# A deformable convolution's sampling loop: TensorE samples between its two distance products, and reads copied offsets

## The chip, the cores and the metric

The kernel runs on one core of one Trainium2 chip. The metric is the device time of one execution in microseconds (us), from the first to the last instruction of the core and what lies around them. TensorE (PE), VectorE (DVE), ScalarE (ACT), GpSimd (POOL) and SyncE (SP) run their own streams of instructions and wait for each other on semaphores.

## The reference

The input is 8 images of 64 channels and 32 x 32 pixels. Two deformable convolutions with 3 x 3 taps come first, then a windowed attention and a mixture of experts. The change touches the two deformable convolutions only:

```python
def deform_conv(x, offset, weight, stride, pad, dil):          # dil = 2, pad = 2
    dy = offset[:, 0::2]
    dx = offset[:, 1::2]
    ...
    ys = base_y[None, None, :, None] + (ky * dil)[None, :, None, None] + dy
    xs = base_x[None, None, None, :] + (kx * dil)[None, :, None, None] + dx
    ...                                   # four neighbours, weighted by the fractions of ys and xs
    return jnp.einsum('oik,bikhw->bohw', weight.reshape(Co, Ci, KK), sampled)
off1 = conv2d(x, w_off1, b_off1, stride=1, pad=1)
out = jax.nn.relu(bn_inf(deform_conv(x, off1, w_dc1, 1, 2, 2), g1, beta1, m1, v1))
off2 = conv2d(out, w_off2, b_off2, stride=1, pad=1)
out = bn_inf(deform_conv(out, off2, w_dc2, 1, 2, 2), g2, beta2, m2, v2)
out = jax.nn.relu(out + x)
```

A bilinear sample at a fractional place is a sum over source pixels with the weight (1 - |y distance|) (1 - |x distance|), where that is positive. The kernel computes it so, as a matrix product.

## The kernel before, in words

**Stages.** Convolution 1, convolution 2, layer norm, attention, layer norm, experts. Each deformable convolution first computes its 18 offsets per pixel on PE (line 548). The offsets are split in three bf16 parts, written to memory and read back (lines 610 and 616) into a buffer `off` with the layout that the sampling wants, in two halves of 16 image rows; the semaphores `moved[0]` and `moved[1]` tell of them. If no offset is as large as 2 pixels (a flag that all engines load), the sampler below runs.

**The sampler.** The source is cut in tiles of 4 x 8 pixels: 8 tile rows (TR) by 4 tile columns. A hardware loop of 8 iterations on PE (line 180) takes one tile row each, and inside it nine steps are written out, one per tap. ACT, DVE and POOL have the same work written out without a loop. A step on PE issues:

- **x**, `columns_near` (line 130): four matmuls that turn the offsets of a tap into x distances of each pixel from a tile's columns. ACT takes their absolute value from PSUM (line 247), DVE makes min(|d|, 1) - 1 of it (line 312).
- **y**, `rows_near` (line 149): two matmuls for the y distances; ACT line 256, DVE line 315.
- **S**, the sampling (line 214): 32 matmuls of 32 source pixels by 64 output channels, each recorded in two passes, so 64 records. The moving operand is `s`, the product of the two hats that DVE makes in two pieces (line 327).
- **w**, `weighted_near` (line 111): the source pixels times the weights of three taps, the stationary operand of S; ACT copies it out of PSUM (line 238). Only the steps 0, 4, 5, 6, 7 and 8 of nine have a w.

Steps run ahead: step t makes x and y of tap t+2. x, y and w pass through two PSUM slots in turn, so the k-th of them waits until ACT has emptied the (k-2)-th. On DVE the order per tap n is fixed: hat of x(n+1), hat of y(n+1), then the two products `s` of tap n (function `sampler_dve`, `hats(n + 1)` and then `weights(n)`). Before step 0 of an iteration PE clears four banks of output (line 195), after ACT has copied the previous tile row's sums (line 297) and DVE has added them to `tokens` (line 351); convolution 2 has a further DVE pass there (line 1332).

**Names.** `emptied` counts ACT's passes, `s_ready` DVE's products, `sampled` the S groups, `staged` POOL's copies of source tiles (line 374). Ten items (x and y of the taps 0 and 1, and the first x of others) are made before the loop, after both `moved` waits.

Of the kernel before, what the change touches and what calls it, by code (L numbers as in the profile page):

```python
# [17 lines left out]
P = 128  # L18
# [99 lines left out]
def columns_near(nc, m, cv, k, tap, row, n, i=None):  # L118

    _, cols, ahead = window(cv)  # L120
    kx = tap % 3
    for late in range(2):
        wide = 2 * cv.reach if late else TILE_COLS
        first = tap * PIX + row * W + ahead - 2 * kx + TILE_COLS * late
        for g in range(2):
            src = m.off_flat[:, first:first + n * W] if i is None else tile_rows(m.off_flat, first, n, i)
            src = src.rearrange("p (r c w) -> p r c w", c=TC, w=TILE_COLS) if i is None else src.rearrange(
                "p r (c w) -> p r c w", c=TC)
            dst = slot_banks(m, k)[:, g, 0:n * TC * cols].rearrange("p (r c w) -> p r c w", c=TC, w=cols)
            last = nc.tensor.matmul(dst[:, :, :, TILE_COLS * late:TILE_COLS * late + wide],  # L130
                                    m.near_sel[:, 6 + ((ahead * 3 + kx) * 2 + late) * 2 + g, :], src[:, :, :, 0:wide],
# [4 lines left out]
def tile_rows(off_flat, first, n, i):  # L136

    room = (TAPS * PIX + OFF_TAIL - first) // W * W
    return off_flat[:, first:first + room].rearrange("p (r c) -> p r c", c=W)[:, bass.ds(i * TILE_ROWS, n), :]

def rows_near(nc, m, cv, k, tap, row, i=None):

    n = window(cv)[0]
    first = tap * PIX + row * W
    for g in range(2):
        src = m.off_flat[:, first:first + n * W] if i is None else tile_rows(m.off_flat, first, n, i)
# [8 lines left out]

# [1619 lines left out]
```

## Time and profile before

| | us |
|---|---|
| median of 3 runs | 966.86 |
| lowest and highest | 961.87, 967.53 |
| profiled execution | 967.68 |
| its span | 965.7 |
| convolution 1, first S to last S | 208.4 |
| convolution 2, first S to last S | 267.9 |

The profile is one execution. An engine's busy time counts instructions and not waits; matmul ends are modelled and overlap the next start, so the distance between two starts tells what a group costs. A line of the timeline gives start, duration, engine, source line, what is written and read, and in brackets how long the engine had been idle and what ended it. The granted clock is 1.00 at 2.4 GHz and 0.50 at 1.2 GHz. The two sampling loops are the same code and take 208.4 and 267.9 us.

### The profile page before, as it was taken

To read this page: it belongs to the slowest core of one execution; us is meant where nothing else is said; L and a number is where in the kernel's file an instruction comes from. 1 tells how busy PE (TensorE), PEld (TensorE's weight loads), DVE (VectorE), ACT (ScalarE), POOL (GpSimd) and SP (SyncE) were. 2 spreads that over 40 slices of the span, in tenths; PEclk is the share of its full clock that TensorE was granted. 3 is DMA by queue.
4 is the path that set the end of the run, shared out by engine and by line. 5 is a ranking of instruction groups with operands and counts; after the bars stand their busy time and mean duration, and the time that the engine had idled before them with its cause. 6 is when DMAs were issued, how large, how long until landed. Compare 5 with 4: busy or idle time off the path is not lost.

```text
span 965.7 us, 39200 instructions
## 1 busy us (share of the span) xinstructions
PE 744.0 (77%) x17378; PEld 563.6 (58%) x17378; DVE 538.7 (56%) x993; ACT 452.1 (47%) x750; POOL 166.6 (17%) x200
## 2 busy tenths in 40 slices
PE   6477777777685676676676676699999999999546
PEld 2255555555423454354354345589999999999434
DVE  2465666656534445445455456346666666666843
ACT  1355556565634544444353453335554444454441
POOL 4000000000000000000000003244444444443210
PEclk8789999999997977888887896789999999999779
DMA  8400000000022000000000006100000000000002
GB/s 208 89 4 1 0 1 0 0 1 0 2 41 37 5 3 5 5 4 5 4 4 4 4 5 157 45 1 2 1 0 0 0 0 0 0 0 0 1 0 89
DMA packets 8146, 17.56 MB, mean 18 GB/s; under 512 B 2149, under 2 KB 6117, under 8 KB 7605
## 3 DMA queue, kind: packets, MB, share of 16 engines
q1 hardware_dynamic: 8022, 15.74, 6.6%
q8 instruction: 98, 1.61, 0.7%
q14 instruction: 26, 0.21, 0.1%
HBM read 11.87 MB, written 3.87 MB: 16 GB/s over the span
## 4 chain that ended last, share of the span: by engine, by line
PE 65%; ACT 13%; DVE 9%; issue 8%; DMA 3%; POOL 1%; SPq 1%; ACTq 0%; DVEq 0%
PE banks L214 13%; PE banks L111 9%; ACT y L238 7%; PE banks L778 7%; PE banks L762 6%; PE banks L808 6%; PE banks L149 5%; PE banks L548 4%; PE banks L819 3%; DVE s L327 3%; PE banks L798 3%; ACT hy L256 2%; PE banks L773 2%; PE banks L195 2%; PE banks L130 2%
## 5 line engine op out<-in xcount | busy, mean ns | idle before, releaser
L214 PE MATMUL banks<-s,y 32*64 32x96 f32 (+2 forms) x9216 | 155.6, 262 | 20.0 <-DVE s L327 16.9
L214 PEld LDWEIGHTS banks<-s,y 32*64 32x64 f32 x9216 | 130.2, 141 | 65.0 <-DVE s L327 39.1
L238 ACT COPY y<-banks 128x768 f32<-128x768 f32 x106 | 84.4, 800 | 153.3 <-PE banks L111 153.3
L327 DVE TENSOR_TENSOR s<-hy,y 128x384 f32<-128x384 f32 x288 | 146.8, 552 | 0.1
L312 DVE TENSOR_SCALAR y<-y 128x384 f32<-128x384 f32 x144 | 51.7, 359 | 150.9 <-ACT y L247 150.8
L149 PE MATMUL banks<-off,near_sel 128*128 (+1 forms) x296 | 63.2, 299 | 75.5 <-ACT y L238 64.8
L247 ACT ACTIVATE y<-banks 128x384 f32<-128x384 f32 x160 | 78.3, 493 | 78.6 <-PE banks L130 77.7
L256 ACT ACTIVATE hy<-banks,row_bias 128x512 f32<-128x512 f32 x148 | 101.6, 686 | 22.1 <-PE banks L149 22.0
L374 POOL COPY stage<-src 128x128 f32<-128x128 f32 x72 | 18.9, 306 | 497.0 <-PE banks L111 497.0
L111 PE MATMUL banks<-w_dc,stage 64*32 64x192 f32 x3392 | 98.5, 343 | 4.5 <-ACT y L238 4.5
L130 PE MATMUL banks<-off,near_sel 128*128 (+2 forms) x640 | 60.7, 225 | 48.5 <-issue 28.4
L876 ACT COPY hy<-banks 128x512 f32<-128x512 f32 x64 | 37.7, 589 | 115.9 <-PE banks L808 115.9
L130 PEld LDWEIGHTS banks<-off,near_sel 128*128 128x128 f16 x640 | 40.8, 105 | 87.6 <-issue 80.8
L315 DVE TENSOR_SCALAR hy<-hy 128x512 f32<-128x512 f32 x144 | 61.5, 427 | 53.7 <-ACT hy L256 53.1
L980 POOL TENSOR_TENSOR y<-y,stats 128x1024 f32<-128x1024 f32 x33 | 62.8, 1903 | 143.7 <-DVE stats L921 143.7
L762 PE MATMUL banks<-src,s 128*128 (+1 forms) x560 | 75.3, 279 | 1.1 <-ACT src L699 1.1
L911 DVE TENSOR_REDUCE stats<-banks 128x16 f32<-128x1024 f32 x34 | 41.6, 1225 | 57.5 <-PE banks L778 57.4
L778 PEld LDWEIGHTS banks<-src,y 128*128 128x128 f32 x544 | 68.9, 199 | 5.4 <-issue 0.6
L762 PEld LDWEIGHTS banks<-src,s 128*128 128x128 f32 x560 | 69.4, 196 | 1.5 <-ACT src L699 1.5
L149 PEld LDWEIGHTS banks<-off,near_sel 128*128 128x128 f16 x296 | 17.7, 100 | 88.6 <-issue 84.7
L778 PE MATMUL banks<-src,y 128*128 128x128 f32 x544 | 68.9, 282 | 0.0
L808 PE MATMUL banks<-y,hy 128*128 128x128 f32 x512 | 67.7, 275 | 0.0
(147 smaller groups left out, 1015.7 us busy)
## 6 DMA issues: line engine op xcount, KB each, us to landing
src<-in_x_dram SPq DMA_DIRECT2D x4, 578.0 KB, 5.8
y<-in_w_dram SPq DMA_DIRECT2D x1, 2080.0 KB
off<-in_w_dram SPq DMA_DIRECT2D x2, 1024.0 KB
out_dram<-tokens SPq DMA_DIRECT2D x4, 512.0 KB, 2.6
offsets_dram<-tokens SPq DMA_DIRECT2D x32, 54.0 KB
off<-offsets_dram SPq DMA_DIRECT2D x16, 108.0 KB
near_sel<-in_near_sel_dram SPq DMA_DIRECT2D x1, 960.0 KB
w_dc<-in_w_dc_dram SPq DMA_DIRECT2D x2, 288.0 KB, 10.3
```

The source lines that it names most:

```text
L111: last = nc.tensor.matmul(m.ps[32 * j:32 * j + 32, FIRST_BANK + 2 * (k % 2) + g, (col % 2) * 192:(col % 2) * 192 + 192], m.stage[rows, ima ...
L130: last = nc.tensor.matmul(dst[:, :, :, TILE_COLS * late:TILE_COLS * late + wide], m.near_sel[:, 6 + ((ahead * 3 + kx) * 2 + late) * 2 + g, ...
L149: last = nc.tensor.matmul(dst if i is None else dst.rearrange("p (r c) -> p r c", c=W), m.near_sel[:, tap // 3 * 2 + g, :], src, start=Tru ...
L214: last = nc.tensor.matmul(out[:, r0:r0 + n, first:first + width], m.yk[32 * j:32 * j + 32, ky, g, col, kx * C:(kx + 1) * C], s_rows(m, cv, ...
L238: nc.scalar.copy(m.yk[:, ky, :, 2 * part:2 * part + 2, :].rearrange("p g a n -> p g (a n)"), slot_banks(m, k)[:, :, 0:384]).then_inc(cv.em ...
L247: nc.scalar.activation(block, slot_banks(m, k)[:, :, 0:n * cols].rearrange("p g (r n) -> p g r n", n=cols), ACT.Abs).then_inc(cv.emptied, 1)
L256: nc.scalar.activation(y_rows(m, cv, n).rearrange("p r g c -> p g r c"), slot_banks(m, k)[:, :, 0:rows * W].rearrange("p g (r c) -> p g r ...
L327: nc.vector.tensor_tensor(dst.rearrange("p r g (a c) -> p (r g) a c", a=TC), y, x.rearrange("p r g (a c) -> p (r g) a c", a=TC), ALU.mult) ...
L762: last = nc.tensor.matmul(m.ps[:, hg, h * P:(h + 1) * P], at.a_heads[:, hg * H4 + h, :], at.xh[:, bass.ds(i + b // BLOCKS, 1), first:first ...
L778: last = nc.tensor.matmul(m.ps[:, 2 + bank, first:first + 2 * KEYS], at.g[:, b % 2, hg, j, :], at.pair_windows[:, b % 2, j, :, :], start=F ...
L808: last = nc.tensor.matmul(m.ps[:, 6, j * P:(j + 1) * P], at.xw[:, b % 2, image, j, :], at.pt[:, image, j * P:(j + 1) * P], start=True, sto ...
L980: nc.gpsimd.tensor_tensor(p, p, scale.unsqueeze(2).to_broadcast([P, 2 * TILES * HG, KEYS]), ALU.mult).then_inc(at.probs_ready, 1)
```

## The change

Five edits, all in the sampler:

1. PE's step is x, S, y, w in place of x, y, S, w.
2. POOL copies the window of offsets that a step needs (3 to 8 rows with a margin) into a small buffer `near_off`, nine copies per tile row. PE waits for them (`off_near`). The addresses of x and y no longer depend on the loop's counter, so the address instructions for them go.
3. x and y read 20 rows of one 32-row group each, where they read all 128 partitions with zeros in the selecting operand. The selecting operand halves (30 to 15 versions).
4. w makes 64 x 64 tiles: 8 matmuls where there were 16 of 64 x 32. The images are assigned to partitions in another order, and `stage` is laid out for it.
5. PE and the flag no longer wait for `moved`; POOL waits for `moved[0]` before its first copy, and for `moved[1]` before the first that needs rows of the second half. ACT waits for the offsets' write-out before it overwrites that memory, in tile row 0.

```diff
-IMAGES = [[0, 1, 2, 3], [5, 4, 7, 6]]
+IMAGES = [[0, 2, 1, 3], [5, 7, 4, 6]]
-OFF_TAIL = 160
+OFF_HEAD, OFF_TAIL = 16, 160
+MARGIN = 4
-VERSIONS, NEAR_VERSIONS = 17, 30
+VERSIONS, NEAR_VERSIONS = 17, 15
...
 def weighted_near(nc, m, cv, k, ky, part):
     for col in (2 * part, 2 * part + 1):
-        for j in range(4):
+        for half in range(2):
             for g in range(2):
-                image = IMAGES[g][j]
+                image = IMAGES[g][2 * half]
                 rows = slice(C * (image % 2), C * (image % 2) + C)
                 last = nc.tensor.matmul(
-                    m.ps[32 * j:32 * j + 32, FIRST_BANK + 2 * (k % 2) + g, (col % 2) * 192:(col % 2) * 192 + 192],
-                    m.stage[rows, image // 2, col, :], cv.w_dc[rows, 3 * ky:3 * ky + 3, :],
-                    start=True, stop=True, skip_group_check=True)
+                    m.ps[C * half:C * half + C, FIRST_BANK + 2 * (k % 2) + g, (col % 2) * 192:(col % 2) * 192 + 192],
+                    m.stage[rows, col, 2 * g:2 * g + 2, :].rearrange("p a n -> p (a n)"),
+                    cv.w_dc[rows, 3 * ky:3 * ky + 3, :], start=True, stop=True, skip_group_check=True)
...
-def rows_near(nc, m, cv, k, tap, row, i=None):
+def rows_near(nc, m, cv, k, tap):
     n = window(cv)[0]
-    first = tap * PIX + row * W
     for g in range(2):
-        src = m.off_flat[:, first:first + n * W] if i is None else tile_rows(m.off_flat, first, n, i)
-        dst = slot_banks(m, k)[:, g, 0:n * W]
-        last = nc.tensor.matmul(dst if i is None else dst.rearrange("p (r c) -> p r c", c=W),
-                                m.near_sel[:, tap // 3 * 2 + g, :], src, start=True, stop=True, skip_group_check=True)
+        part = group_rows(g, 0)
+        last = nc.tensor.matmul(slot_banks(m, k)[:, g, 0:n * W], m.near_sel[part, tap // 3, :],
+                                m.near_off[part, tap, MARGIN:MARGIN + n * W], start=True, stop=True,
+                                skip_group_check=True)
     last.then_inc(cv.filled, 1)
...
 def sampler_pe(nc, pe, m, cv):
     old = 2 * cv.reach
-    for half in range(HALVES):
-        pe.wait_ge(cv.moved[half], MOVES)
     for k, item in enumerate(FIRST_COORDS, len(FIRST_WEIGHTED)):
         kind, tap, tile_row = item
         pe.wait_ge(cv.emptied, k - 1)
+        pe.wait_ge(cv.off_near, tap + 1)
...
         for t in range(TAPS):
-            later, tap = divmod(t + AHEAD, TAPS)
+            tap = (t + AHEAD) % TAPS
             pe.wait_ge(cv.emptied, i * PER_ROW + (k - 1))
-            columns_near(nc, m, cv, k, tap, new_rows(cv, tap) + TILE_ROWS * later, TILE_ROWS, i)
-            k += 1
-            pe.wait_ge(cv.emptied, i * PER_ROW + (k - 1))
-            rows_near(nc, m, cv, k, tap, first_row(cv, tap) + TILE_ROWS * later, i)
+            pe.wait_ge(cv.off_near, i * TAPS + (t + AHEAD + 1))
+            columns_near(nc, m, cv, k, tap, old, TILE_ROWS)
             k += 1
...
-            if t in STEP_WEIGHTED:
-
-                pe.wait_ge(cv.emptied, i * PER_ROW + (k - 1))
-                if STEP_WEIGHTED[t] == (0, 0, 1):
-                    pe.wait_ge(cv.staged, i * PAIRS + 2 * PAIRS)
...
             last.then_inc(cv.sampled, 1)
+            pe.wait_ge(cv.emptied, i * PER_ROW + (k - 1))
+            if t in STEP_WEIGHTED:
+
+                pe.wait_ge(cv.emptied, i * PER_ROW + k)
+                if STEP_WEIGHTED[t] == (0, 0, 1):
+                    pe.wait_ge(cv.staged, i * PAIRS + 2 * PAIRS)
+            rows_near(nc, m, cv, k, tap)
+            k += 1
             if t in STEP_WEIGHTED:
                 weighted_near(nc, m, cv, k, *STEP_WEIGHTED[t][0:2])
...
 def sampler_pool(nc, pool, m, cv):
-    for tile_row in range(1, TR + 1):
-        pool.wait_ge(cv.filled, EMPTIED_AT["w", 2, 1, tile_row - 1])
-        stage_pool(nc, m, cv, min(tile_row, TR - 1))
+    rows = window(cv)[0]
+    moved = 0
+    for n in range(TR * TAPS + AHEAD):
+        tile_row, tap = divmod(n, TAPS)
+        if tile_row:
+            pool.wait_ge(cv.filled, EMPTIED_AT["y", tap, tile_row - 1])
+        row = TILE_ROWS * tile_row + first_row(cv, tap)
+        first = row * W - MARGIN
+        left_out = max(-first, 0)
+        if moved == 0 or moved == 1 and row + rows >= HALF_ROWS:
+            pool.wait_ge(cv.moved[moved], MOVES)
+            moved += 1
+        at = OFF_HEAD + tap * PIX + first
+        size = rows * W + 2 * MARGIN
+        nc.gpsimd.tensor_copy(m.near_off[:, tap, left_out:size], m.off_flat[:, at + left_out:at + size]
+                              ).then_inc(cv.off_near, 1)
+        if tap == AHEAD - 1 and tile_row:
+            pool.wait_ge(cv.filled, EMPTIED_AT["w", 2, 1, tile_row - 1])
+            stage_pool(nc, m, cv, min(tile_row, TR - 1))
...
+                if cv.k == 0:
+                    nc.gpsimd.memset(m.near_off[:, :, :], 0.0).then_inc(near_cleared, 1)
+                    pool.wait_ge(near_cleared, 1)
...
-                pe.wait_ge(cv.moved[0], MOVES)
                 pe.wait_ge(cv.flag_ready, 1)
```

ACT's and DVE's instructions and their order stay as they were. On PE, step 4 of an iteration (a step with a w) stood so before, from its y to the x of step 5:

```order
L149 ISA [waits c0_emptied]
L149 MATMUL banks<-off,near_sel 128x256 x2
L199 REGISTER_ALU
L201 REGISTER_ALU [waits c0_emptied]
L205 REGISTER_ALU [waits c0_staged]
L214 MATMUL banks<-s,y 64x8x10 [waits c0_s_ready]
L214 MATMUL banks<-s,y 64x8x10 x7
L214 MATMUL banks<-s,y 64x8x12 x16
L214 MATMUL banks<-s,y 64x8x10 x8
L111 MATMUL banks<-w_dc,stage 32x192 x16
L184 REGISTER_ALU
L130 ISA [waits c0_emptied]
```

The same place of the changed kernel (L195 is S now, L141 is y, L112 is w):

```order
L130 MATMUL banks<-near_off,near_sel 128x16x4 x2
L186 REGISTER_ALU
L195 MATMUL banks<-s,y 64x8x10 [waits c0_s_ready]
L195 MATMUL banks<-s,y 64x8x10 x7
L195 MATMUL banks<-s,y 64x8x12 x16
L195 MATMUL banks<-s,y 64x8x10 x8
L200 REGISTER_ALU
L203 REGISTER_ALU [waits c0_emptied]
L205 ISA [waits c0_emptied]
L141 MATMUL banks<-near_off,near_sel 128x256 [waits c0_staged]
L141 MATMUL banks<-near_off,near_sel 128x256
L112 MATMUL banks<-w_dc,stage 64x192 x8
```

The y that stood ahead of S stands behind it, with the waits that S had, and w has half the instructions.

On DVE the order per tap is the same in both. In the changed kernel (L305 is the hat of x, L308 the hat of y, L320 the products `s`), in the loop's first steps:

```order
L305 TENSOR_SCALAR y<-y 128x384 [waits c0_emptied]
L308 TENSOR_SCALAR hy<-hy 128x512 [waits c0_emptied]
L320 TENSOR_TENSOR s<-hy,y 128x384 [waits c0_hats,c0_sampled]
L320 TENSOR_TENSOR s<-hy,y 128x384
L305 TENSOR_SCALAR y<-y 128x384 [waits c0_emptied]
```

The products of tap n stand behind the hat of y(n+1), as before.

## Rows read from the trace of the kernel before

**Rows 1.** Waits of PE in the whole execution: waiting line, releaser, total us, times, longest.

```profile
PE banks L149 <- ACT y L238: 64.8, 81, 0.8
PE banks L130 <- issue: 28.4, 7, 4.3
```

**Rows 2.** Busy time per engine, first S to last S of each convolution; PEclk is the granted clock.

```profile
53.07:261.46 208.39, 158.79 (x6503) 109.31 (x6503) 125.62 (x286) 121.40 (x201) 8.40 (x32) 0.99 0.00 1
307.25:575.16 267.91, 185.87 (x6504) 123.19 (x6503) 134.05 (x310) 121.57 (x201) 8.40 (x32) 0.84 0.02 4
```

**Rows 3.** Timeline of a step with a w in convolution 1: start, us, engine, line.

```profile
122.36 0.39 PE L149 MATMUL banks<-off,near_sel 128*128 x2 [0.82 <-ACT y L238]
...
122.74 0.99 PE L214 MATMUL banks<-s,y 32*64 32x96 f32 x64
122.78 0.69 ACT L256 ACTIVATE hy<-banks,row_bias 128x512 f32<-128x512 f32 x1 [0.17 <-PE banks L149]
123.50 0.43 DVE L315 TENSOR_SCALAR hy<-hy 128x512 f32<-128x512 f32 x1 [0.50 <-ACT hy L256]
...
123.66 0.88 PE L111 MATMUL banks<-w_dc,stage 64*32 64x192 f32 x32
123.85 1.02 DVE L327 TENSOR_TENSOR s<-hy,y 128x384 f32<-128x384 f32 x2
...
124.47 0.35 PE L130 MATMUL banks<-off,near_sel 128*128 x4
```

**Rows 4.** Timeline, end of a step without a w in convolution 1.

```profile
115.09 1.02 DVE L327 TENSOR_TENSOR s<-hy,y 128x384 f32<-128x384 f32 x2
...
116.17 0.99 PE L214 MATMUL banks<-s,y 32*64 32x80 f32 x64 [0.60 <-DVE s L327]
```

**Rows 5.** Timeline, boundary of two tile rows in convolution 1.

```profile
130.34 0.59 ACT L297 COPY tokens<-banks 128x512 f32<-128x512 f32 x1 [0.30 <-PE banks L214]
131.03 1.22 DVE L351 TENSOR_TENSOR tokens<-tokens,banks 128x1024 f32<-128x1024 f32 x1 [0.53 <-ACT tokens L297]
...
132.16 1.02 DVE L327 TENSOR_TENSOR s<-hy,y 128x384 f32<-128x384 f32 x2
...
133.24 1.00 PE L214 MATMUL banks<-s,y 32*64 32x96 f32 x64
```

**Rows 6.** Timeline, the same boundary in convolution 2.

```profile
401.65 1.22 DVE L351 TENSOR_TENSOR tokens<-tokens,banks 128x1024 f32<-128x1024 f32 x1 [0.59 <-ACT tokens L297]
...
403.96 1.02 DVE L327 TENSOR_TENSOR s<-hy,y 128x384 f32<-128x384 f32 x2
```

**Rows 7.** Timeline, start of convolution 1's sampler, and POOL's first copies in its loop.

```profile
30.20 2.46 SPq L616 DMA_DIRECT2D off<-offsets_dram  x4
...
44.70 0.80 PE L130 MATMUL banks<-off,near_sel 128*128 128x128 bf16 x8 [9.82 <-DMA off<-offsets_dram]
...
55.94 1.05 POOL L374 COPY stage<-src 128x128 f32<-128x128 f32 x4 [42.25 <-PE banks L111]
```

**Rows 8.** Timeline, start of convolution 2's sampler.

```profile
284.37 2.17 SPq L616 DMA_DIRECT2D off<-offsets_dram  x4
...
292.11 2.25 SPq L616 DMA_DIRECT2D off<-offsets_dram  x4
292.25 0.15 DVE L330 COPY prime<-b_off 128x1 f32<-128x1 f32 x1 [1.02 <-issue]
...
298.96 0.80 PE L130 MATMUL banks<-off,near_sel 128*128 128x128 bf16 x8 [8.22 <-DMA off<-offsets_dram]
```

**Rows 9.** PE's timeline in convolution 2, granted clock at its lower level.

```profile
378.82 1.50 PE L214 MATMUL banks<-s,y 32*64 32x80 f32 x64
380.25 0.50 PE L130 MATMUL banks<-off,near_sel 128*128 x4
```

**Rows 10.** Busy time and granted clock of two stretches of the last layer norm.

```profile
897.70:905.30 7.60, 3.00 (x24) 2.58 (x24) 6.08 (x9) 1.06 (x1) 0.00 (x0) 1.00 0.00 0
905.40:918.90 13.50, 7.24 (x31) 6.07 (x32) 10.30 (x15) 7.40 (x10) 5.80 (x4) 0.50 0.01 2
```

More of the change, by code:

```diff
@@ L106, in weighted_near, with columns_near @@
     for col in (2 * part, 2 * part + 1):
-        for j in range(4):
+        for half in range(2):
             for g in range(2):
-                image = IMAGES[g][j]
+                image = IMAGES[g][2 * half]
                 rows = slice(C * (image % 2), C * (image % 2) + C)
                 last = nc.tensor.matmul(
-                    m.ps[32 * j:32 * j + 32, FIRST_BANK + 2 * (k % 2) + g, (col % 2) * 192:(col % 2) * 192 + 192],
-                    m.stage[rows, image // 2, col, :], cv.w_dc[rows, 3 * ky:3 * ky + 3, :],
-                    start=True, stop=True, skip_group_check=True)
+                    m.ps[C * half:C * half + C, FIRST_BANK + 2 * (k % 2) + g, (col % 2) * 192:(col % 2) * 192 + 192],
+                    m.stage[rows, col, 2 * g:2 * g + 2, :].rearrange("p a n -> p (a n)"),
+                    cv.w_dc[rows, 3 * ky:3 * ky + 3, :], start=True, stop=True, skip_group_check=True)
     last.then_inc(cv.filled, 1)
-def columns_near(nc, m, cv, k, tap, row, n, i=None):
-    _, cols, ahead = window(cv)
+def columns_near(nc, m, cv, k, tap, row, n):
+    rows, cols, ahead = window(cv)
     kx = tap % 3
@@ L123, in columns_near @@
         wide = 2 * cv.reach if late else TILE_COLS
[L124 removed]
+        first = MARGIN + row * W + ahead - 2 * kx + TILE_COLS * late
         for g in range(2):
[L126 to L128 removed]
+            part = group_rows(g, 1)
+            src = m.near_off[part, tap, first:first + n * W].rearrange("p (r c w) -> p r c w", c=TC, w=TILE_COLS)
             dst = slot_banks(m, k)[:, g, 0:n * TC * cols].rearrange("p (r c w) -> p r c w", c=TC, w=cols)
             last = nc.tensor.matmul(dst[:, :, :, TILE_COLS * late:TILE_COLS * late + wide],
[L131 removed]
+                                    m.near_sel[part, 3 + (ahead * 3 + kx) * 2 + late, :], src[:, :, :, 0:wide],
                                     start=True, stop=True, skip_group_check=True)
     last.then_inc(cv.filled, 1)
[L136 to L142 removed]
+def rows_near(nc, m, cv, k, tap):
     n = window(cv)[0]
[L145 removed]
     for g in range(2):
[L147 to L150 removed]
+        part = group_rows(g, 0)
+        last = nc.tensor.matmul(slot_banks(m, k)[:, g, 0:n * W], m.near_sel[part, tap // 3, :],
+                                m.near_off[part, tap, MARGIN:MARGIN + n * W], start=True, stop=True,
+                                skip_group_check=True)
     last.then_inc(cv.filled, 1)
@@ L155, in first_row @@
     return window(cv)[2] - 2 * (tap // 3)
-def new_rows(cv, tap):
-    return first_row(cv, tap) + 2 * cv.reach
 def s_rows(m, cv, n):
@@ L218, in sampler_pe @@
             last.then_inc(cv.sampled, 1)
+            pe.wait_ge(cv.emptied, i * PER_ROW + (k - 1))
[3 more added lines that the diff above has]
+                    pe.wait_ge(cv.staged, i * PAIRS + 2 * PAIRS)
+            rows_near(nc, m, cv, k, tap)
+            k += 1
             if t in STEP_WEIGHTED:
@@ L293, in sampler_act @@
                 if t == TAPS - 1 and kind == "w" and tile_row < TR - 1:
+                    if tile_row == 0:
+                        for half in range(HALVES):
+                            for g in range(2):
+                                act.wait_ge(cv.bounced[half][g], 64)
                     act.wait_ge(cv.sampled, TAPS * (tile_row + 1))
@@ L1695, in constants @@
     near = np.zeros((4, 32, NEAR_VERSIONS, P), f16)
-    for g in range(2):
-        for ky in range(3):
-            near[2 * g, 0:ROWS_OFF, ky * 2 + g] = sel[2 * g, :, 2 - ky]
-        for ahead in range(2):
-            for kx in range(3):
-                for late in range(2):
-                    version = near[2 * g + 1, :, 6 + ((ahead * 3 + kx) * 2 + late) * 2 + g]
-                    version[0:PARTS] = sel[2 * g + 1, 0:PARTS, 0]
-                    version[ROW_MOD + ahead * 3 + kx] = 1
-                    version[ROW_ONE] = ahead - 2 + TILE_COLS * late - pixel % TILE_COLS
+    for ky in range(3):
+        near[0::2, 0:ROWS_OFF, ky] = sel[0::2, :, 2 - ky]
+    for ahead in range(2):
+        for kx in range(3):
+            for late in range(2):
+                version = near[1::2, :, 3 + (ahead * 3 + kx) * 2 + late]
+                version[:, 0:PARTS] = sel[1::2, 0:PARTS, 0]
+                version[:, ROW_MOD + ahead * 3 + kx] = 1
+                version[:, ROW_ONE] = ahead - 2 + TILE_COLS * late - pixel % TILE_COLS
     c["near_sel"] = near.reshape(P, NEAR_VERSIONS, P)
```

19 lines of the change are left out of this document (10 added, 9 removed).

## The prediction, made before the changed kernel was run

> **What bounds the kernel now.** I read the waits first, then the stretches of the two sampling loops, then the timeline of single steps. PE waits longest for ACT's pass over w: y has to wait until the slot of the previous w is empty, 81 times and 64.8 us in all [rows 1]. That is the wait that the change is aimed at. The reader should then see that the two loops, which are the same code, differ by 59.5 us (208.4 and 267.9) and that convolution 2 alone moves instructions by DMA and has a granted clock of 0.84 [rows 2]. PE waits there for nothing that the profile shows, 28.4 us in 7 turns of up to 4.3: once at the end of each iteration [rows 1]. So convolution 1's loop is bound by the turns between PE, ACT and DVE, and convolution 2's by these and by a stall at the loop's end. In a step with a w, DVE's products start at 123.85 and the next S comes well behind them, held by PE's own row of waits; in a step without a w, S starts as soon as DVE has made `s`: from the start of the products to S 1.08 us [rows 3, 4].
>
> **The new order closes a loop through four engines.** S of tap t waits for the products of tap t. On DVE these stand behind the hat of y(t+1). That y is issued in step t-1, and there it now stands behind S(t-1). So from S to S the path is: S(t-1), y(t+1), ACT's pass, DVE's hat, DVE's products, S(t), with nothing of it overlapping. Before, y(t+1) stood ahead of S(t-1) and this path ran beside it. Its pieces: from the start of S to the next group on PE 0.92 (122.74 to 123.66); from y to ACT's pass 0.42 (122.36 to 122.78); from there to the hat 0.72 (to 123.50); hat to products 0.35 (to 123.85); products to S 1.08 [rows 3, 4]. Sum 3.49 us. The two matmuls of y now use different groups of 32 rows. The 64 records of S in 0.92 us, 14 ns apart though each streams 64 to 96 columns, show that matmuls on different row groups do run together here [rows 3]; then the pair saves one of its two passes of 256 columns, 0.11 us at 2.4 GHz (an estimate; the pair's record is 0.39 in all, so it is bounded by 0 and 0.11; I take 0.11, since S is the nearest row). The step is then 3.38 us, bounds 3.38 and 3.49. 
> w (0.81 from 123.66 to 124.47 before, [rows 3]) and x now lie in the 2.5 us in which PE waits for DVE, so the halved w, the shorter x and the saved address instructions are worth nothing on the path. If that cover were gone they would be worth at most the 0.81 of w in 6 steps of 9. POOL's nine copies per tile row: four copies of 128 elements take 1.05 us [rows 7], so one of 264 at most twice 0.26, nine of them 4.8 us of a tile row of 30, and each has a whole tile row's time. Nothing. The one clearing of the new buffer stands before convolution 1's first source copy, over 40 us before POOL is next wanted [rows 7]: nothing.
>
> **Boundary of tile rows.** Six times per convolution DVE adds sums before the products. ACT's copy for it now stands behind ACT's pass over the late y: S to y 0.92, y to ACT 0.31, that pass 0.69, then copy to add 0.69 (130.34 to 131.03), add to products 1.13, products to S 1.08: 4.82 us. In convolution 2 add to products is 2.31 (401.65 to 403.96), which makes 6.00 [rows 3, 5, 6].
>
> **Sum of the loops, clock at the upper level.** 71 intervals from first S to last S: 65 x 3.38 + 6 x 4.82 = 248.6 in convolution 1, against 208.4: **+40.2**. 219.7 + 6 x 6.00 = 255.7 in convolution 2, against 267.9: **-12.2** [rows 2]. The second holds that the stall at the loop's end goes. Convolution 1's copy of this loop runs without it and without DMA [rows 2], so it comes from where the loop lies in PE's instructions and how long it is; the change takes 96 matmul records and as many weight loads of 826 each out of an iteration, an eighth. I take it that it then fits in both places. With the upper bound of the step the two sums are 7.2 us larger each (65 of 0.11).
>
> **Starts.** The second half of the offsets is issued from 292.11 and PE's first x starts at 298.96, 6.85 later [rows 8]. The first half is issued from 284.37, so it is there at about 291.2, before the flag, after which DVE starts at 292.25. With a POOL copy of 0.5 PE can start at about 292.8: **-6.2**. In convolution 1 the first half is issued at 30.20, there at about 37.1 to 38 (the queue is busier), against a start at 44.70: **-6.8** [rows 7]. Together -13.0. The ten items before the loop are paced by ACT as before.
>
> 967.7 + 40.2 - 12.2 - 13.0 = 982.7 with the clock at its upper level; 997.1 with the larger step.
>
> **The clock.** With the new order PE is idle for some 2 us before each S of a step without a w: S, y and x are about 1.4 us of 3.4. Before, in convolution 1, its work was 158.8 of 208.4 us at 0.99 [rows 2]. The nearest stretch with such a pattern is the last layer norm: 3.0 us of work in 7.6, in bursts of 1 to 2 us, at 1.00; directly after it the granted clock was 0.50, and stayed there for 13.5 us though PE then had 7.2 us of work [rows 10]. So I expect it to fall (from 2.4 to 1.2 GHz) in the three steps of each tile row without a w and at the boundary, and to rise again in the five steps with a w, in which PE works for more than two thirds of the step. At the lower level S takes 1.43 instead of 0.92 (378.82 to 380.25, [rows 9]), one pass of y 0.11 more: 0.62 per step. I choose 4 such steps per tile row in convolution 1 and 5 in convolution 2 (its boundary is idle for longer), 72 of 142: **+44.6**. Ends: none, and all 142 with 88 us. 982.7 + 44.6 = 1027; with the larger step 1042. Between the two: **1032 us**. The profiled execution (967.7) stands 0.8 above the median of 966.9, which is less than anything here resolves.
>
> **Rivals.**
> - *The clock stays up.* For it: the five steps with a w lie close, and the work in those without is spread in bursts every 3.4 us, where the layer norm had idle stretches of 2. Against: rows 10. Time 983 to 997. Chance 0.21.
> - *The clock stays down in nearly all steps.* In convolution 2 the mean was 0.84 although PE worked for 185.9 of 267.9 us [rows 2]. Time 983 + 88 to 997 + 105: 1071 to 1102. Chance 0.09.
> - *The instruction stall stays in convolution 2.* It would hold PE for 4.2 us where the boundary is now idle for about 2 of them, and clock losses follow: 7 x 2.2 and some 8 for the clock, 24 us on the forecast, 1056. The Trainium skill, "Runtime: NRT & Kernel Launch", section Instruction fetch mechanics, has a rule for it: a taken branch out of the current window forces a fetch, and PE's instruction memory holds 2048 instructions. Convolution 1, whose seven jumps back show no instruction traffic [rows 2], agrees with the second part, and a shorter loop is the better off. Chance 0.08.
> - *Faster.* The loop through y is shorter than its pieces, each measured where something else may have overlapped: the same sum equals 967.7 when a step is 0.11 us shorter than 3.38 (15 us over 142), that is 3.27, and gives 943 at 3.10, with the clock up. It needs ACT to start within 0.1 us of y's issue, or the products to start before the hat of y ends. Against: 3.38 has every saving in it that I can name, and the clock must not fall once. Chance 0.06.
> - The forecast, 1005 to 1060: chance 0.56.
>
> **Range and chances.** What a measurement tells from no change is about 1%, 10 us. Faster than that needs the last rival: 0.06. Within 1%, 957 to 977: its slow end and the fast end of the first: 0.06. Slower by more: 0.88. The range leaves out the faster half of what is below 980 and the slow half of the second rival: 979 to 1080.
>
> **What would show it.** The distance from S to S in convolution 1 with the clock at 1.00: 3.4 us in all steps, with or without a w, where it was 3.28 and 1.7 to 2.3. PE's wait for ACT at y gone (64.8 us) and in its place 1.8 to 2.5 us before each S, released by DVE. Convolution 2 without instruction DMA in the loop and without the waits of 4 us. The granted clock falling in each tile row of both loops. First x at about 38 us in convolution 1. I am wrong if S starts without waiting for DVE, if the clock stays at 1.00, or if the two loops still differ by 60 us.

## The result and the profile after

| | before | after |
|---|---|---|
| median, us | 967.2 (4 runs) | 1041.8 (4 runs) |
| lowest and highest | 961.9, 978.1 | 1039.1, 1045.6 |
| profiled execution | 967.68 | 1045.62 |
| its span | 965.7 | 1043.6 |
| convolution 1, first S to last S | 208.4 | 277.7 |
| convolution 2, first S to last S | 267.9 | 288.2 |

The changed kernel is **slower**: ratio 1.0794, interval 1.0733 to 1.0855. Every ratio here is of fast executions alone and leaves out the slow ones, as the 978.1 us of the kernel before. The forecast was 1032, range 979 to 1080.

PE's waits of the changed kernel (waiting line, releaser, total us, times, longest; S is L195, the clearing of the output banks L181, x L130):

```profile
PE banks L195 <- DVE s L320: 162.9, 132, 2.2
PE banks L181 <- DVE tokens L344: 10.6, 7, 1.5
...
PE banks L130 <- POOL near_off L372: 4.7, 4, 2.2
```

Both waits of [rows 1] are gone: ACT's pass over w no longer holds y (64.8 us), and the 28.4 us of "issue" at x no longer stand in the list. In their place S waits for DVE's products 132 times, 162.9 us in all.

The two sampling loops by windows (PE, PEld, DVE, ACT, POOL busy; granted clock; DMA share; GB/s):

```profile
43.52:321.18 277.66, 187.63 (x5752) 125.51 (x5751) 127.92 (x288) 120.39 (x201) 40.83 (x95) 0.67 0.00 1
360.50:648.69 288.19, 197.84 (x5752) 131.43 (x5751) 133.53 (x312) 119.85 (x201) 38.51 (x95) 0.62 0.00 0
```

Against [rows 2] the two are nearly alike now. Convolution 2's DMA share is 0.00 where it was 0.02, and the granted clock fell from 0.99 to 0.67 and from 0.84 to 0.62. The page has the clock and the instruction queue in one row each:

```profile
PEclk8856656785678866585575576589999999999768
...
q8 instruction: 33, 0.54, 0.2%
```

Before, q8 had moved 98 packets and 1.61 MB.

A step at the upper clock, in convolution 1's third tile row (start, us, engine, line; in brackets how long the engine had been idle and what ended it). It answers to [rows 3, 4]:

```profile
118.91 0.99 PE L195 MATMUL banks<-s,y 32*64 32x80 f32 x64 [1.28 <-DVE s L320]
119.84 0.28 PE L141 MATMUL banks<-near_off,near_sel 20*128 20x256 bf16 x2
...
120.16 0.69 ACT L245 ACTIVATE hy<-banks,row_bias 128x512 f32<-128x512 f32 x1 [1.53 <-PE banks L141]
...
120.88 0.43 DVE L308 TENSOR_SCALAR hy<-hy 128x512 f32<-128x512 f32 x1 [1.65 <-ACT hy L245]
121.22 1.02 DVE L320 TENSOR_TENSOR s<-hy,y 128x384 f32<-128x384 f32 x2
...
122.30 1.50 PE L195 MATMUL banks<-s,y 32*64 32x64 f32 x64 [2.18 <-DVE s L320]
```

These six lines hold the whole loop, each starting when the one above lets it: S, 0.93, y, 0.32, ACT, 0.72, hat, 0.34, products, 1.08, S. That is 3.39 us. The S at 122.30 is already at the lower clock (1.50 for 0.99), as in [rows 9], and so are the next steps, 4.00 us each:

```profile
126.31 1.50 PE L195 MATMUL banks<-s,y 32*64 32x96 f32 x64 [2.18 <-DVE s L320]
127.74 0.40 PE L141 MATMUL banks<-near_off,near_sel 20*128 20x256 bf16 x2
...
128.18 0.69 ACT L245 ACTIVATE hy<-banks,row_bias 128x512 f32<-128x512 f32 x1 [2.94 <-PE banks L141]
...
130.31 1.50 PE L195 MATMUL banks<-s,y 32*64 32x80 f32 x64 [2.18 <-DVE s L320]
```

S to y grows from 0.93 to 1.43 and y to ACT from 0.32 to 0.44, together 0.62; nothing else in the loop is PE's.

The boundary of two tile rows, against [rows 5]:

```profile
110.57 1.00 PE L195 MATMUL banks<-s,y 32*64 32x64 f32 x64 [0.42 <-DVE s L320]
...
111.50 0.28 PE L141 MATMUL banks<-near_off,near_sel 20*128 20x256 bf16 x2
...
111.82 0.69 ACT L245 ACTIVATE hy<-banks,row_bias 128x512 f32<-128x512 f32 x1 [0.63 <-PE banks L141]
...
112.41 0.58 ACT L290 COPY tokens<-banks 128x512 f32<-128x512 f32 x1
...
113.09 1.22 DVE L344 TENSOR_TENSOR tokens<-tokens,banks 128x1024 f32<-128x1024 f32 x1
...
114.22 1.02 DVE L320 TENSOR_TENSOR s<-hy,y 128x384 f32<-128x384 f32 x2
...
115.30 1.00 PE L195 MATMUL banks<-s,y 32*64 32x96 f32 x64
```

4.73 us from S to S: ACT's copy of the sums stands behind its pass over the late y.

The start of convolution 1's sampler, against [rows 7]:

```profile
36.25 3.54 POOL L372 COPY near_off<-off 128x260 bf16<-128x260 bf16 x10 [20.94 <-DMA off<-offsets_dram]
...
36.80 0.61 PE L130 MATMUL banks<-near_off,near_sel 20*128 20x128 bf16 x8 [2.18 <-POOL near_off L372]
...
43.52 1.50 PE L195 MATMUL banks<-s,y 32*64 32x96 f32 x64
```

x starts 7.9 us earlier than before (44.70), the first S 9.55 earlier (53.07).

**Account of the profiled executions.** 1045.62 less 967.68 is 77.9 us: start of convolution 1 -9.55, its loop +69.3 (277.66 less 208.39), start of convolution 2 -6.5 (39.3 from last S to first S, 45.8 before), its loop +20.3 (288.19 less 267.91), everything behind the last S +4.4 (394.9 for 390.5). They sum to 77.9 within the rounding.

### The profile page after: what moved, and what is told of

The parts are those of the page before. It is cut to its first block, busy times and chain, and to the rows that moved or that the text cites. A ratio compares the mean times of both kernels' runs of the same rounds, so it can differ in the third digit from the quotient of the medians.

```text
span 1043.6 us, 35691 instructions
## 1 busy us (share of the span) xinstructions
PE 786.3 (75%) x15682; PEld 584.9 (56%) x15682; DVE 539.9 (52%) x993; ACT 450.1 (43%) x750; POOL 239.3 (23%) x349
## 4 chain that ended last, share of the span: by engine, by line
PE 58%; DVE 20%; ACT 13%; issue 7%; POOL 1%; DMA 1%; SPq 0%; POOLq 0%; DVEq 0%; ACTq 0%
PE banks L195 18%; DVE s L320 13%; ACT hy L245 9%; PE banks L787 6%; PE banks L771 6%; PE banks L817 5%; PE banks L141 4%; PE banks L557 3%; PE banks L828 3%; PE banks L807 3%; PE banks L782 2%; PE banks L798 1%; PE banks L112 1%; PE banks L181 1%; DVE tokens L344 1%
## 5 line engine op out<-in xcount | busy, mean ns | idle before, releaser
L195 PE MATMUL banks<-s,y 32*64 32x96 f32 (+2 forms) x9216 | 192.0, 320 | 163.2 <-DVE s L320 162.9
L195 PEld LDWEIGHTS banks<-s,y 32*64 32x64 f32 x9216 | 161.2, 182 | 197.4 <-DVE s L320 196.6
L308 DVE TENSOR_SCALAR hy<-hy 128x512 f32<-128x512 f32 x144 | 61.6, 428 | 264.1 <-ACT hy L245 264.1
L372 POOL COPY near_off<-off 128x264 bf16<-128x264 bf16 (+3 forms) x148 | 60.1, 413 | 390.1 <-PE banks L141 341.1
L320 DVE TENSOR_TENSOR s<-hy,y 128x384 f32<-128x384 f32 x288 | 148.6, 558 | 0.1
L112 PE MATMUL banks<-w_dc,stage 64*64 64x192 f32 x1696 | 131.2, 444 | 4.1 <-ACT y L227 4.1
L112 PEld LDWEIGHTS banks<-w_dc,stage 64*64 64x64 f32 x1696 | 71.1, 177 | 34.6 <-issue 15.1
L305 DVE TENSOR_SCALAR y<-y 128x384 f32<-128x384 f32 x144 | 52.8, 366 | 37.2 <-ACT y L236 36.6
L771 PEld LDWEIGHTS banks<-src,s 128*128 128x128 f32 x560 | 69.3, 196 | 1.5 <-ACT src L708 1.5
L787 PEld LDWEIGHTS banks<-src,y 128*128 128x128 f32 x544 | 66.7, 193 | 5.2 <-issue 0.3
L787 PE MATMUL banks<-src,y 128*128 128x128 f32 x544 | 66.7, 276 | 0.0
L817 PEld LDWEIGHTS banks<-y,hy 128*128 128x128 f32 x512 | 62.3, 192 | 0.0
L928 DVE TENSOR_REDUCE stats<-y 128x16 f32<-128x1024 f32 x34 | 41.4, 1218 | 36.0 <-ACT y L872 36.0
L130 PE MATMUL banks<-near_off,near_sel 20*128 20x64 bf16 (+1 forms) x640 | 49.4, 245 | 8.4 <-POOL near_off L372 4.7
```

The costliest lines, as they stand in the source:

```text
L112: last = nc.tensor.matmul(m.ps[C * half:C * half + C, FIRST_BANK + 2 * (k % 2) + g, (col % 2) * 192:(col % 2) * 192 + 192], m.stage[rows, ...
L195: last = nc.tensor.matmul(out[:, r0:r0 + n, first:first + width], m.yk[32 * j:32 * j + 32, ky, g, col, kx * C:(kx + 1) * C], s_rows(m, cv, ...
L308: nc.vector.tensor_scalar(y, y, *hat).then_inc(cv.hats, 1)
L320: nc.vector.tensor_tensor(dst.rearrange("p r g (a c) -> p (r g) a c", a=TC), y, x.rearrange("p r g (a c) -> p (r g) a c", a=TC), ALU.mult) ...
L372: nc.gpsimd.tensor_copy(m.near_off[:, tap, left_out:size], m.off_flat[:, at + left_out:at + size]).then_inc(cv.off_near, 1)
L771: last = nc.tensor.matmul(m.ps[:, hg, h * P:(h + 1) * P], at.a_heads[:, hg * H4 + h, :], at.xh[:, bass.ds(i + b // BLOCKS, 1), first:first ...
```

## The experiments

Each run is compared with the kernel before on the same chip. "Steps at the lower clock" are the S groups longer than 1.25 us in the profile, of 144.

**The order alone.** The kernel before, with y and the waits of the w step moved behind S and nothing else:

```diff
-            pe.wait_ge(cv.emptied, i * PER_ROW + (k - 1))
-            rows_near(nc, m, cv, k, tap, first_row(cv, tap) + TILE_ROWS * later, i)
-            k += 1
...
             last.then_inc(cv.sampled, 1)
+            pe.wait_ge(cv.emptied, i * PER_ROW + (k - 1))
+            if t in STEP_WEIGHTED:
+                pe.wait_ge(cv.emptied, i * PER_ROW + k)
...
+            rows_near(nc, m, cv, k, tap, first_row(cv, tap) + TILE_ROWS * later, i)
+            k += 1
```

> The kernel before with one edit of the change alone: y behind S. Theory: every step about 3.5 us (the pair of y in turn, 0.1 more than in the changed kernel) and 4.1 at the lower clock, convolution 1 about 285 us, convolution 2 about 310 to 320, since the instruction stall at each iteration's end stays; the starts stay as before. 967 + 77 + 48 = about 1090, slower than the changed kernel. Rival, the order is not the loss: under 1000.

Measured: 1079.6 us, ratio 1.1095 (1.1017 to 1.1172). Steps of 3.49 us at the upper and 4.21 at the lower level, 28 + 39 of them at the lower one. 3.49 is the forecast's sum before its saving of 0.11. The stall in convolution 2 stays:

```profile
PE banks L206 <- DVE s L326: 149.1, 126, 2.0
PE banks L130 <- issue: 24.0, 7, 3.6
```

So the new order alone costs more than the whole change, and the rest of the change gives some of it back.

**The change with the old order.** The changed kernel, y ahead of S again; all other edits stay:

```diff
             columns_near(nc, m, cv, k, tap, old, TILE_ROWS)
             k += 1
+            pe.wait_ge(cv.emptied, i * PER_ROW + (k - 1))
+            rows_near(nc, m, cv, k, tap)
+            k += 1
...
             last.then_inc(cv.sampled, 1)
-            pe.wait_ge(cv.emptied, i * PER_ROW + (k - 1))
...
-            rows_near(nc, m, cv, k, tap)
-            k += 1
```

> The changed kernel with one edit undone: y stands ahead of S again, all else (copied offsets, 20-row selection, 64x64 w, earlier start) stays. Theory, the loss is the loop S, y, ACT, hat, products, S: the steps go back to 3.28 with a w and 1.7 to 2.3 without, S is released by the products 1.1 us after their start, the clock stays at 1.00, convolution 1 takes 200 to 209 us from first S to last S, convolution 2 about 7 more (its boundary pass), so 1041.8 - 69 - 72 = about 900. Rival, the copies, the 20-row matmuls or the w tiles cost it: it stays above 1000.

Measured: 958.5 us, ratio 0.9842 (0.9743 to 0.9941). The theory of the order holds: at the upper clock S to S is back at 3.24 with w and about 3.0, 2.45 and 1.54 without, and PE again waits for ACT at y (70.6 us). But the time is 58 us above what I expected. The clock is the reason: 39 + 37 steps are still at the lower level (convolution 1 and 2), and 38 of these 76 are steps with a w that take 4.42 for 3.24 us, 45 us together. PE's rows of this kernel, first a step at the lower level, then one at the upper level three steps later (S is L202):

```profile
118.08 1.49 PE L202 MATMUL banks<-s,y 32*64 32x64 f32 x64
119.50 1.56 PE L112 MATMUL banks<-w_dc,stage 64*64 64x192 f32 x16
120.99 0.34 PE L130 MATMUL banks<-near_off,near_sel 20*128 20x128 bf16 x4
122.03 0.39 PE L141 MATMUL banks<-near_off,near_sel 20*128 20x256 bf16 x2 [0.70 <-ACT y L226]
122.50 1.50 PE L202 MATMUL banks<-s,y 32*64 32x96 f32 x64
...
131.34 0.99 PE L202 MATMUL banks<-s,y 32*64 32x64 f32 x64 [0.18 <-ACT y L235]
132.27 0.88 PE L112 MATMUL banks<-w_dc,stage 64*64 64x192 f32 x16
133.08 0.26 PE L130 MATMUL banks<-near_off,near_sel 20*128 20x128 bf16 x4
```

At the lower level S to w is 1.42 for 0.93 and w to x 1.49 for 0.81. Here w is on the path, so a step loses 1.18 and not 0.62. The w of half as many matmuls is not shorter: from w to x it is 0.81 us, as in the kernel before [rows 3]. What lowered the clock, though y is ahead of S as in the kernel before? Two edits changed PE's work in a step: w in half as many matmuls, and x and y on 20 rows.

**The same with x and y on all 128 partitions**, the selecting operand with its zeros as before:

```diff
-        last = nc.tensor.matmul(slot_banks(m, k)[:, g, 0:n * W], m.near_sel[part, tap // 3, :],
-                                m.near_off[part, tap, MARGIN:MARGIN + n * W], start=True, stop=True,
+        last = nc.tensor.matmul(slot_banks(m, k)[:, g, 0:n * W], m.near_sel[:, tap // 3 * 2 + g, :],
+                                m.near_off[:, tap, MARGIN:MARGIN + n * W], start=True, stop=True,
```

(x likewise.)

> e1_order_back (changed kernel, y ahead of S) with x and y reading all 128 partitions again, from the copied offsets. Question: in e1 the granted clock fell in every tile row, though PE's groups follow each other as in the kernel before, where it was 1.00 throughout. Theory A, it fell because x and y use 20 rows of the array in place of 128: the clock is back at 1.00 in both loops, about 26.4 us per tile row, total about 900 to 905. Theory B, it fell because of w in half as many, larger matmuls: the clock falls as in e1, total about 955.

Measured: 912.3 us, ratio 0.9393 (0.9327 to 0.9460). The two loops, of the run with 20 rows first and of this one second:

```profile
43.81:281.16 237.35, 180.71 (x5751) 121.63 (x5751) 131.33 (x287) 120.96 (x202) 38.05 (x95) 0.73 0.00 1
319.37:561.20 241.83, 178.49 (x5752) 120.04 (x5751) 139.11 (x311) 120.84 (x202) 37.91 (x95) 0.75 0.00 1
```

```profile
45.45:254.34 208.89, 156.97 (x5752) 108.94 (x5751) 127.34 (x287) 121.33 (x202) 38.99 (x95) 1.00 0.00 1
293.25:513.46 220.21, 164.29 (x5752) 114.10 (x5751) 134.86 (x311) 121.31 (x202) 39.03 (x95) 0.95 0.00 1
```

The order is the same and so are the instructions but for the rows that x and y read, and the granted clock goes from 0.73 to 1.00 and from 0.75 to 0.95, with 76 steps at the lower level against 11. In convolution 1 the loop takes 208.9 us, what it took before (208.4, [rows 2]): with the order and the rows as before, the halved w, the fewer address instructions and POOL's copies are worth nothing. What the runs don't separate is whether the rows count or the time: on 20 rows x and y are also shorter on PE (their groups 0.26 and 0.28 us for 0.34 and 0.39 at the upper clock).

**The same with the old w**, 16 matmuls of 64 x 32 and the old `stage` in place of 8 of 64 x 64 (x and y on 20 rows, y ahead of S):

```diff
-        for half in range(2):
+        for j in range(4):
...
-                    m.ps[C * half:C * half + C, FIRST_BANK + 2 * (k % 2) + g, (col % 2) * 192:(col % 2) * 192 + 192],
+                    m.ps[32 * j:32 * j + 32, FIRST_BANK + 2 * (k % 2) + g, (col % 2) * 192:(col % 2) * 192 + 192],
```

> e1_order_back with w in 16 matmuls of 64x32 and the old assignment of images, x and y still on 20 rows. Theory A (x and y on 20 rows pull the clock down): the clock falls as in e1, total about 955. Theory B (w pulls it down): 1.00 in both loops, about 900 to 905.

Measured: 987.8 us, ratio 1.0141 (1.0070 to 1.0211). The profiled execution took 999.8 us, so I read only its pattern: 38 + 50 steps at the lower clock, in convolution 1 one fewer than with the halved w. The granted clock of its other three executions is 0.81 to 0.84, with the halved w 0.83 to 0.84, and on 128 partitions 0.93 or 0.94. So w is not what lowered it; x and y on 20 rows are. And the stall of [rows 1] is back:

```profile
PE banks L130 <- issue: 28.4, 7, 4.4
...
q8 instruction: 98, 1.61, 0.8%
```

**Is the stall one of place?** The kernel before, with 37 matmuls ahead of convolution 2's loop that are never executed (they stand in the branch for far offsets, which is not taken). No instruction that runs differs:

```diff
+    if cv.k == 0:
+        for _ in range(37):
+            nc.tensor.matmul(m.ps[:, 0, :], m.zeros[:, 0:P], m.zeros[:, :], start=True, stop=True,
+                             skip_group_check=True)
```

> The kernel before, with 37 matmuls (74 instructions) put into the branch for far offsets of convolution 1, which is never taken: nothing that is executed changes, only the place of convolution 2's loop in PE's instructions. Theory, the stall of 4.2 us at each iteration's end in convolution 2 comes from where the loop of 1717 instructions lies: it goes, boundaries fall from 9.5 to 5.1 us, no instruction traffic in the loop, the clock stays at 1.00, convolution 2 takes about 216 us from first S to last S in place of 267.9, total about 915. Rival, the stall belongs to convolution 2's code or data: 967, unchanged.

Measured: 927.4 us, ratio 0.9548 (0.9484 to 0.9612), by 74 instructions that are never executed.

```profile
311.39:528.59 217.20, 161.51 (x6504) 111.15 (x6503) 132.57 (x310) 121.28 (x201) 8.39 (x32) 0.97 0.00 1
...
q8 instruction: 34, 0.56, 0.3%
```

Convolution 2 takes 217.2 for 267.9 us [rows 2], its boundary 5.1 us, and 0.97 of the clock is granted for 0.84. So of the 59.5 us between the two loops 50.7 were a stall that comes from where the loop lies, with its clock losses; the longer boundary (1.2 us, 6 times, [rows 5, 6]) is most of the rest. The loop's length in the built program is 1717 instructions before, about 1700 with the old w put back and 1507 in the changed kernel: the two longer ones stall in convolution 2, and the shorter doesn't. The Trainium skill, "Runtime: NRT & Kernel Launch", Instruction fetch mechanics, gives blocks of 256 instructions and 2048 in all for PE. By that and the built addresses the loop before touches 7 blocks in convolution 1 and 8 in convolution 2, and the others that don't stall at most 7, so a loop seems to be held if it touches 7, though 8 blocks are just the 2048 that the page gives. How the blocks lie against the program's first instruction no run shows. That the place decides is shown; the count of blocks is argued from addresses and one shift.

**DVE's order.** If the loop through y is the cost because products(n) stand behind the hats of n+1, then exchanging them opens it. The changed kernel, with that alone:

```diff
-        if n + 1 < TR * TAPS:
-            hats(n + 1)
...
         weights(n)
+        if n + 1 < TR * TAPS:
+            hats(n + 1)
```

> The changed kernel with VectorE's order turned: the products of tap n before the hats of tap n+1, so that y(t+1), issued behind S(t-1), is wanted only for S(t+1). Theory: the loop through four engines then spans two steps, a step is bound by PE (w 0.81, S 0.92, x and y 0.45: 2.2 us) or DVE (1.8 us), convolution 1 about 165 to 180 us, convolution 2 about 7 more, the clock near 1.00, total about 825 to 850. Rival, another turn closes at the same length (the two PSUM slots and ACT's passes over w and x): steps stay above 3 us and the time above 960.

Measured: 891.2 us, ratio 0.9171 (0.9088 to 0.9253). S to S is 2.46 with w (before: 3.28) and 1.44 to 2.5 without. The steps at the lower clock (32 + 41, with w 3.51) keep it above what I expected.

**Fill the idle time.** The changed kernel with 4 (in steps with w) or 8 matmuls of zeros between x and S, which add zero to the output:

```diff
             columns_near(nc, m, cv, k, tap, old, TILE_ROWS)
             k += 1
+            for bank in range(PAIRS):
+                for _ in range(1 if t in STEP_WEIGHTED else 2):
+                    nc.tensor.matmul(m.ps[:, bank, 0:OUT_ROWS * W], m.zeros[:, 0:P], m.zeros[:, 0:OUT_ROWS * W],
+                                     start=False, stop=True, skip_group_check=True)
```

> The changed kernel with matmuls of zeros onto the output banks (four of 384 columns in a step with a w, eight in one without) between x and S, where PE only waits for VectorE; they add zero. Theory, the clock falls because PE idles there: it stays at 1.00 in both loops, every step is 3.4 us, 97 S of the lower level lose 0.62 us each, total about 980 to 985. Rival, the clock is not what makes the odd steps 4.0 us, or the fillers delay S: 1030 or more.

Measured: 1000.0 us, ratio 1.0291 (1.0226 to 1.0355). Nearly all steps away from the boundaries are 3.39 us; 4 + 7 are at the lower clock:

```profile
120.77 1.00 PE L199 MATMUL banks<-s,y 32*64 32x96 f32 x64 [0.78 <-DVE s L324]
121.69 0.28 PE L141 MATMUL banks<-near_off,near_sel 20*128 20x256 bf16 x2
121.73 0.26 PE L130 MATMUL banks<-near_off,near_sel 20*128 20x128 bf16 x4
121.92 0.82 PE L185 MATMUL banks<-zeros 128*128 128x384 f16 x4
124.15 0.99 PE L199 MATMUL banks<-s,y 32*64 32x80 f32 x64 [1.41 <-DVE s L324]
```

4% of the time come back by work that computes nothing. It stays above what I expected because at a boundary the fillers also stand between the clearing and S: 5.23 or, after an idle time that lowered the clock, 6.08 us for 4.73 there, and then 3.67 or 4.2 for the next step.

**Only the rows, with y still behind S.** The changed kernel with the 128 partitions of above and nothing else (x and y as shown there):

```diff
-VERSIONS, NEAR_VERSIONS = 17, 15
+VERSIONS, NEAR_VERSIONS = 17, 30
```

> The changed kernel with x and y reading all 128 partitions again, y still behind S. Theory: y's two passes run in turn, so every step is 0.1 us longer (3.49 and 4.2), which costs 14 us; the clock falls for fewer steps than the 94 of the changed kernel, because the reads of 20 rows no longer pull it down; the order alone still makes PE idle 2 us in a step without a w, so that some 50 to 65 steps stay at the lower clock. Total 1025 to 1040. Rival, the row count was the whole cause of the lower clock: below 1000.

Measured: 1044.1 us, ratio 1.0753 (1.0688 to 1.0819): no difference from the change that is clear of noise. 24 + 37 steps are at the lower clock for 97, but a step is 3.49 and 4.21 for 3.39 and 4.01. 36 x 0.62 is 22 us gained, and what the longer steps give up is 142 x 0.10 plus 61 x 0.10, 20 us. Set beside the run with the order alone, which has the same order and rows, it also prices the other edits under the late y: 3.49 and 4.21 us in both, with w in 8 or 16 matmuls.

**Both, and the boundary.** DVE's exchange together with 128 partitions:

```diff
-VERSIONS, NEAR_VERSIONS = 17, 15
+VERSIONS, NEAR_VERSIONS = 17, 30
...
         weights(n)
+        if n + 1 < TR * TAPS:
+            hats(n + 1)
```

> e3_dve_swap with x and y reading all 128 partitions. Theory A: the steps at the lower clock (3.5 with a w in place of 2.46) go, a step costs 0.1 us more for y's two passes in turn, total 835 to 850. Theory B: as e3, 891, or a little slower.

Measured: 862.2 us, ratio 0.8855 (0.8792 to 0.8918), 5 + 11 steps at the lower clock, 2.57 us with w. Then ACT copies a tile row's sums ahead of its pass over the late y, not behind it:

```diff
-                if t == TAPS - 1 and kind == "w" and tile_row < TR - 1:
+                if t == TAPS - 1 and kind == "y" and tile_row < TR - 1:
```

> e9_swap_rows128 with one more edit: at the end of a tile row ScalarE copies the sums out of PSUM before its pass over the late y, not after it. Theory: the copy starts 1.0 us after S in place of 1.9, the boundary falls from 4.95 to about 4.1 us in convolution 1 and from 6.13 to about 5.2 in convolution 2, 14 of them 13 us, and some of the S at the lower clock behind the boundary go: 845 to 850. Rival, the boundary is bound by PE's clearing of the banks or by its instructions: within 3 us of e9's 862.

Measured: 842.0 us (840.1 to 845.5, 6 runs), ratio 0.8666 (0.8627 to 0.8706). The boundary is 3.93 and 5.11 us for 4.95 and 6.13. It is the fastest of all and beats both kernels.

```profile
45.19:219.71 174.52, 157.96 (x5752) 111.05 (x5751) 131.31 (x286) 120.84 (x201) 47.79 (x95) 1.00 0.00 1
258.08:444.03 185.95, 162.90 (x5751) 113.74 (x5750) 138.57 (x311) 120.28 (x201) 46.14 (x95) 0.96 0.00 1
```

One of its steps (y is L139, DVE's products L318, the hat that this y feeds L306):

```profile
157.29 1.00 PE L193 MATMUL banks<-s,y 32*64 32x96 f32 x64
...
157.94 1.02 DVE L318 TENSOR_TENSOR s<-hy,y 128x384 f32<-128x384 f32 x2
158.22 0.39 PE L139 MATMUL banks<-near_off,near_sel 128*128 128x256 bf16 x2
...
159.37 0.43 DVE L306 TENSOR_SCALAR hy<-hy 128x512 f32<-128x512 f32 x1
...
159.74 0.99 PE L193 MATMUL banks<-s,y 32*64 32x80 f32 x64
```

The products for the S at 159.74 start 0.28 us ahead of the y that they once waited for.

**The runs side by side** (ratio to the kernel before; in brackets the steps at the lower clock):

| | x, y on 20 rows | on 128 partitions |
|---|---|---|
| y ahead of S, DVE as before | 0.9842 (76) | 0.9393 (11) |
| y behind S (the change: left) | 1.0794 (97) | 1.0753 (61) |
| y behind S, products ahead of hats | 0.9171 (73) | 0.8855 (16) |

## Why the prediction was right, and where it was off

**The loop through four engines: shown.** The forecast's step was 3.38 us, measured 3.39; its bound without the saving was 3.49, measured 3.49 where x and y keep all partitions. The cause is shown from both sides: y ahead of S takes it away (0.9842), and DVE's exchange too (0.9171), and the order alone makes it in the old kernel (1.1095). The saving of 0.11 by two row groups that run together was right: y to ACT fell from 0.42 to 0.32. The drain that the Trainium skill, "TensorEngine Tiling (Array Packing)", Key Properties, sets at a change of mode does not show as an addition: S to y is 0.93, where S to w was 0.92 [rows 3]. Both are changes of mode, so a drain can be in either number, and no run separates it.

**Boundary.** Forecast 4.82 and 6.00, measured 4.73 and 5.91, each 0.09 shorter: ACT's copy starts 0.59 behind its pass (111.82 to 112.41), not 0.69.

**The stall of convolution 2: gone, as forecast**, and for the reason given: with the old w it comes back at 28.4 us. That place alone decides it, at any work, is more than I had said. The rival in which it stays is refuted.

**Starts.** Forecast -6.2 in convolution 2 and -6.8 in convolution 1, measured -6.5 and -9.55. In convolution 1 the items ahead of the loop also ran quicker (x to first S 6.7 us for 8.4).

**The clock: it fell as forecast, but stayed down longer.** This is the term that was mis-sized: I took 72 steps at the lower level, the profile has 97 of 144. The price per step was right (0.62, measured 0.61 to 0.62). The 25 more make 15.5 of the 18.6 us by which the profiled 1045.6 lies above the sum of 1027; 4.4 lie behind the last S, -3.0 at the starts, and 1.7 remain. I reasoned from PE's idle time only, and took the clock to rise in the five steps with a w (4 to 8): 50 of these 80 steps are at the lower level. The experiment with y ahead of S and 20 rows has the idle time of before and yet 76 steps at the lower level; on 128 partitions it has 11. With the late y the idle time alone does much of it (61 steps on 128 partitions), and the 20 rows add the other 36; each count is of one profile. That the total came out as near as 1032 is in part luck: I stood between the sums with and without the saving of 0.11, and the saving came.

**The rivals.** "The clock stays up" is refuted by the profile, and the run with fillers shows what it would have given: steps of 3.39 throughout and 1000 us, with boundaries longer than the change's. "Nearly all steps" fell short by a third. "Faster" needed an S with little wait for DVE; the exchange on DVE makes that (PE waits 20.7 us at S for its products, for 162.9), and it was not in the change.

**Covered edits.** That they are worth nothing in the new order is shown by the equal steps of the run with the order alone and the run with only the rows put back, 3.49 and 4.21 us. For the halved w my reason, the cover, is not the whole one: with y ahead of S, where w is on the path, the loops are equal too (208.9 and 208.4 us), since w takes 0.81 us either way. What it was worth is what I had put down to the fewer instructions: it made the loop fit.

**Open.** The 4.4 us behind the last S: PE waits there 3.35 us for nothing shown, at its first matmul groups behind the sampler. Seven of the eight experiments built on the changed kernel have such a wait, 2.6 to 4.3 us; the kernel before, its new order alone and its shift don't. Yet in all ten profiles of the experiments that part takes 392 to 395 us, 392.9 where only 74 dead instructions were added to the kernel before, so the 4.4 are not that wait alone; 390.5 is the one profile of before. And convolution 1's clock in the shifted kernel before (12 steps at the lower level, where the kernel before has 0.99 of the clock in the same loop, [rows 2]) shows that the old order too stands near the edge. Its code and place in convolution 1 are those of the kernel before, so a dozen steps can differ between two profiles of the same loop; what tipped it was not tried.

## What to carry to other kernels

Before an instruction group is moved behind another, follow its result once around through every in-order engine: if the group it now stands behind waits for work that an engine has queued behind the moved group's consumer, the loop's pieces add up; then look at whether that engine's queue, and not the issuing one's, should be reordered. Read TensorE's granted clock together with what a cheaper matmul takes away: an edit that saves work off the path can lower the clock under the work on it. And a stall by "issue" at a loop's end that only one of two equal loops has was here a matter of the loop's place and length; a shorter body, or a shift of its place, is the first thing to try.

## What the runs showed of the hardware that I had not expected

- **x and y on fewer rows came with a lower clock.** On 20 rows or on 128 partitions, the same order, the same number and column counts: granted clock 0.73 or 1.00 in convolution 1, 958.5 or 912.3 us. Whether the rows or the shorter groups do it is open.
- **A wait that returns as a clock.** A step with w at the lower level is 4.42 us for 3.24 with y ahead of S, and 4.01 for 3.39 behind it: the level costs most where PE itself is on the path.
- **A place for a loop.** 74 instructions never executed made the kernel 4.5% faster (ratio 0.9548).
- **POOL's copies beside DVE's products.** POOL's four source copies take 1.98 us in the changed kernel, beside DVE's products, where they took 1.05 [rows 7], and the products beside them 1.24 where they otherwise take 1.02:

```profile
117.42 1.98 POOL L383 COPY stage<-src 128x128 f32<-128x128 f32 x4 [5.16 <-PE banks L112]
...
117.61 1.24 DVE L320 TENSOR_TENSOR s<-hy,y 128x384 f32<-128x384 f32 x2
```

The Trainium skill, "GPSIMD Engine Reference", Specifications, says that the two contend where a VectorE instruction has two inputs in SBUF, as the products have; the trace agrees. The old layout of `stage` isn't the difference: with it and the new order alone they take 1.94 us in convolution 1 too, and the 1.05 are copies beside which DVE ran nothing. In convolution 1 it makes the step after a boundary up to 3.61 us for 3.39, 1.5 us over its eight copies. In convolution 2 six of the eight start 0.48 us behind the products; they take 1.44 and the products 1.02.
